# mLSTM cell inside a fused six-layer block: output banks copied by ScalarE, the causal mask taken out of TensorE's exponents

## The reference, cut to what matters

```
log_fg = log_sigmoid(fg); cs = cumsum(log_fg)
log_D[s, t] = cs[s] - cs_shift[t] + ig[t]      for t <= s, else -inf
D = exp(log_D - max_t log_D)
C = (q k^T / sqrt(DH)) * D
normaliser = max(|sum_t C|, exp(-max_log_D))
h = (C / (normaliser + 1e-8)) v
h_norm = (h - mean) / sqrt(var + 1e-5) * (1 + out_w)
x = layernorm(x + h_norm)
```

## Time and profile before

| | us |
|---|---|
| median of 3 runs | 1833.98 |
| lowest, highest | 1831.88, 1847.02 |
| profiled execution, its own time | 1832.67 |
| its span | 1830.9 |
| busy TensorE / VectorE / ScalarE / GpSimd | 1626.3 / 1176.4 / 683.8 / 312.8 |
| mLSTM unit loop in it, TensorE | 1094.4 to 1167 |
| covariance and bias matmuls | 1167 to 1187 |

### The profile page before, as it was taken

How to read it: one execution, slowest core, us unless ns; L and a number is a source line. 1 busy time by engine, 2 the same in 40 slices (tenths; PEclk the granted TensorE clock), 3 DMA queues, 4 the chain that set the end, 5 groups by cost and what they waited for, 6 DMA issues and landing times. The chain is left out here.

```text
span 1830.9 us, 38607 instructions
## 1 busy us (share of the span) xinstructions
PE 1626.3 (89%) x14748; PEld 1273.9 (70%) x14748; DVE 1176.4 (64%) x3829; ACT 683.8 (37%) x1425; POOL 312.8 (17%) x329
## 2 busy tenths in 40 slices
PE   6899987899997678898988869898899999999998
PEld 4677765666655556677776647776788888788876
DVE  3555664455554725566555636548888889889894
ACT  3333331246555246656555533323222223222210
POOL 1443435200000110000112105601010001000100
PEclk9899998999999868999998986799999999999999
DMA  3100000000010278989989970230000000000000
GB/s 125 47 18 18 18 18 13 18 19 25 25 54 30 87 258 301 327 281 326 319 299 330 333 237 16 95 141 2 1 8 8 13 2 13 13 2 13 2 7 13
DMA packets 98502, 177.36 MB, mean 97 GB/s; under 512 B 16144, under 2 KB 82832, under 8 KB 93584
## 3 DMA queue, kind: packets, MB, share of 16 engines
q1 hardware_dynamic: 98320, 174.89, 27.6%
HBM read 92.94 MB, written 81.79 MB: 95 GB/s over the span
## 5 line engine op out<-in xcount | busy, mean ns | idle before, releaser
L104 PE MATMUL bank<-per_xT,per_down 128*128 128x256 f32 x1024 | 250.5, 390 | 2.3 <-ACT per_xT L2625 1.6
L2946 PE MATMUL bank<-per_up,per_act_w 128*128 128x256 f32 x1024 | 242.3, 382 | 0.0
L2946 PEld LDWEIGHTS bank<-per_up,per_act_w 128*128 128x128 f32 x1024 | 195.3, 191 | 27.0
L2632 ACT ACTIVATE per_act_w<-bank 128x512 f32<-128x512 f32 x128 | 76.3, 598 | 364.0 <-PE bank L104 329.5
L104 PEld LDWEIGHTS bank<-per_xT,per_down 128*128 128x128 f32 x1024 | 190.2, 192 | 29.9 <-issue 2.7
L1503 ACT ACTIVATE rel_probs<-later_shared,rel_low 128x256 f32<-128x256 f32 x256 | 117.0, 518 | 27.4 <-DVE rel_low L1587 27.3
L1587 DVE CUSTOM_DVE_ANT_0 later_shared<-bank,later_shared 128x256 f32<-128x256 f32 x256 | 95.0, 419 | 37.0 <-DMA later_shared<-rel_qr_rows 18.9
L920 DVE TENSOR_REDUCE xat_mx<-bank 128x2 f32<-128x512 f32 x128 | 79.4, 683 | 32.7 <-PE bank L968 32.7
L104 PE MATMUL bank<-ret_x2T,ret_w_in 128*128 128x256 f32 x384 | 93.0, 399 | 7.5 <-issue 7.5
L2612 POOL TENSOR_TENSOR per_sim<-per_sim,per_best_i 128x512 f32<-128x512 f32 x32 | 41.9, 1330 | 332.6 <-DVE per_sim L2750 332.6
L1722 PE MATMUL bank<-rel_band_k,later_shared 32*128 32x191 f32 x512 | 64.6, 374 | 31.1 <-DVE rel_low L1587 23.8
(11 more groups left out here) (362 smaller groups left out, 3194.6 us busy)
## 6 DMA issues: line engine op xcount, KB each, us to landing
rel_qr_rows<-later_shared SPq DMA_DIRECT2D x32, 1024.0 KB, 8.4
rel_p_rows<-rel_probs SPq DMA_DIRECT2D x32, 1024.0 KB, 6.8
later_shared<-rel_qr_rows SPq DMA_DIRECT2D x64, 384.0 KB, 4.7
rel_by_dist<-rel_p_rows SPq DMA_DIRECT2D x64, 384.0 KB, 4.7
per_down<-in_per_down SPq DMA_DIRECT2D x1, 4096.0 KB, 12.8
per_up<-in_per_up SPq DMA_DIRECT2D x1, 4096.0 KB, 13.0
ret_xin<-in_x SPq DMA_DIRECT2D x8, 256.0 KB, 2.8
xat_cT<-in_contextT SPq DMA_DIRECT2D x8, 256.0 KB, 2.9
```

Of the source, the lines that this page charges most:

```text
L104: last = pe.matmul(dst, wt[:, c], src[:, c, :], start=c == 0, stop=c == DC - 1)
L2632: nc.scalar.activation(act_w[m % 2][:, 2 * k:2 * k + 2, :], tiles(bank[3 + k % 2]), ACT.Gelu_apprx_tanh).then_inc(gelu_ready, 1)
L2946: last = pe.matmul(tiles(bank[7])[:, t, :], act_w[n % 2][:, k, t * P:t * P + P], up[:, k, :], start=k == 0, stop=k == COLS - 1)
```

## The change

- The mask: `mask`, `mask16` and `ident16` go, and with them the two mask matmuls of each unit and ScalarE's two conversions. A table `limit` comes in, 3e38 on and below the diagonal and 0 above, and VectorE takes the minimum of decay and limit on the diagonal squares (128x512 a unit, both inputs in SBUF), ahead of line 2192.
- The outputs' banks: ScalarE copies them to `h` in SBUF, one instruction of 128x260 a bank (`take_of`, step 2b + 2), and TensorE's next outputs wait for `h_taken`, bank 6 and bank 7 apart. VectorE's normalisation reads h: its pairs of instructions (one for each bank) become one each, five in all, and it is done in step 2b + 3. All later per-batch steps move by one as well.
- h lies where `v_in` and `v_sum` lay (`values`), whose use is over by then.
- The sixth layer's steps beside the mLSTM layer are moved with it: the centre from step 7 to 9, beta_wide from 9 to 10, the centrings from step 8 and on to 9 and on, the reads of x by one step. BESIDE and STEPS are one step longer.
- The DMAs of the two tables are issued with the gates' (five under one semaphore, in place of three and two).

```diff
@@ mlstm_layer, streams
-    STEPS = range(-1, UNITS + 6)
+    STEPS = range(-1, UNITS + 7)
+    def take_of(s):
+        return batch(s - 2)
     def norm_of(s):
-        return batch(s - 2)
+        return batch(s - 3)
...
@@ scalar
-            if k == 4:
-                act.wait_ge(exact_loaded, 16 * len(exact_loads))
-                nc.scalar.activation(ident16[:], ident[:], ACT.Copy)
-                nc.scalar.activation(mask16[:], mask[:], ACT.Copy)
...
+            if (b := take_of(s)) is not None:
+                act.wait_ge(h_mm, HP * (b + 1))
+                if b >= 2:
+                    act.wait_ge(hn_part, b - 1)
+                for t in range(TT):
+                    nc.scalar.activation(h[:, b % 2, t], h_bank(t), ACT.Copy).then_inc(h_taken, 1)
@@ vector
                 dve.wait_ge(decay_ready, U + 1)
+                own = decay[:, U % 2].rearrange("p k (c s) -> p k c s", s=P)[:, :, 0:3:2]
+                dve.tensor_tensor(own, own, limit[:].unsqueeze(1).broadcast_to([P, HP, 2, P]), ALU.min)
+                dve.drain()
                 dve.wait_ge(qk_mm, U + 1)
...
-                dve.wait_ge(h_mm, HP * (b + 1))
+                dve.wait_ge(h_taken, TT * (b + 1))
...
-                for t in range(TT):
-                    dve.scalar_tensor_tensor(out=norm[:, t], in0=h_bank(t)[:, :, DH], scalar=-1.0,
-                                             in1=percol[:, 1, t, NH * b:NH * b + NH],
-                                             op0=ALU.mult, op1=ALU.max)
+                dve.scalar_tensor_tensor(out=norm[:], in0=h[:, b % 2, :, :, DH], scalar=-1.0,
+                                         in1=percol[:, 1, :, NH * b:NH * b + NH], op0=ALU.mult, op1=ALU.max)
                 dve.drain()
-                for t in range(TT):
-                    dve.tensor_tensor(norm[:, t], h_bank(t)[:, :, DH], norm[:, t], ALU.max)
+                dve.tensor_tensor(norm[:], h[:, b % 2, :, :, DH], norm[:], ALU.max)
...
-                for t in range(TT):
-                    last = dve.tensor_tensor(hn[:, b % 2, t], h_bank(t)[:, :, 0:DH], over(norm[:, t], DH), ALU.mult)
-                last.then_inc(hn_part, 1)
+                dve.tensor_tensor(flat(hn[:, b % 2]), flat(h[:, b % 2])[:, :, 0:DH],
+                                  over(norm[:].rearrange("p t h -> p (t h)"), DH), ALU.mult).then_inc(hn_part, 1)
@@ tensor
             for k in range(HP):
-                pe.matmul(d_bank(U, k)[:, 0:SPAN], minus[:, NH * b + HP * pair + k], m_parts[:],
-                          start=True, stop=False)
-                behind = d_bank(U, k)[:].rearrange("p (t s) -> p t s", t=TT)[:, :, 0:P]
-                last = pe.matmul(behind, ident16[:], mask16[:], start=False, stop=True)
+                last = pe.matmul(d_bank(U, k)[:, 0:SPAN], minus[:, NH * b + HP * pair + k], m_parts[:],
+                                 start=True, stop=True)
...
-            if b >= 1:
-                pe.wait_ge(hn_part, b)
             for k in range(HP):
+                n = HP * pair + k
+                if b >= 1 and n == 0:
+                    pe.wait_ge(h_taken, TT * b - 1)
...
+                if b >= 1 and n == 0:
+                    pe.wait_ge(h_taken, TT * b)
...
@@ peer_layer
-    BESIDE = range(-1, 2 * nb + 6)
+    BESIDE = range(-1, 2 * nb + 7)
...
-            if s >= 8 and s % 2 == 0:
-                if s == 8:
+            if s >= 9 and s % 2 == 1:
+                if s == 9:
                     pool.wait_ge(centre_ready, 1)
...
-            if s == 7:
+            if s == 9:
                 dve.wait_ge(centre_mm, 1)
```

More of the change, by code:

```diff
@@ L1880, in sem @@
         return nc.alloc_semaphore("mls_" + name)
-    mask, diag = early("mask", [TT, P]), early("diag", [R], rows=PARTS)
-    ident16, mask16 = early("ident16", [P], BF16), early("mask16", [TT, P], BF16)
+    limit, diag = early("limit", [TT, P]), early("diag", [R], rows=PARTS)
     w_gate, b_gate = early("w_gate", [3, DC, 2, NH]), early("b_gate", [2], rows=LINES)
@@ L1928, in mlstm_layer @@
                                                   sem("decay_ready"))
-    qk_mm, c_ready, h_mm, hn_part, sq_ready = (sem("qk_mm"), sem("c_ready"), sem("h_mm"), sem("hn_part"),
-                                               sem("sq_ready"))
+    qk_mm, c_ready, h_mm, h_taken, hn_part, sq_ready = (sem("qk_mm"), sem("c_ready"), sem("h_mm"), sem("h_taken"),
+                                                        sem("hn_part"), sem("sq_ready"))
     hvar, hrstd, hn_ready, out_ready, var, rstd, y_ready = (sem("hvar"), sem("hrstd"), sem("hn_ready"),
                                                             sem("out_ready"), sem("var"), sem("rstd"), sem("y_ready"))
-    gate_loads = [(w_gate[:], w["w_gate"]), (b_gate[:], w["b_gate"]), (select[:], w["select"])]
-    exact_loads = [(mask[:], w["mask"]), (diag[:], w["diag"])]
+    gate_loads = [(w_gate[:], w["w_gate"]), (b_gate[:], w["b_gate"]), (select[:], w["select"]),
+                  (limit[:], w["limit"]), (diag[:], w["diag"])]
     rest_loads = [(out_w[:], w["out_w"].partition_broadcast(P))]
-    STEPS = range(-1, UNITS + 6)
+    STEPS = range(-1, UNITS + 7)
     def unit(k):
@@ L1944, in batch @@
         return k // HP if k % HP == 0 and 0 <= k // HP < nb else None
+    def take_of(s):
+        return batch(s - 2)
     def norm_of(s):
-        return batch(s - 2)
+        return batch(s - 3)
     def var_of(s):
-        return batch(s - 3)
+        return batch(s - 4)
     def scale_of(s):
-        return batch(s - 4)
+        return batch(s - 5)
     def stats_of(s):
-        return batch(s - 5)
+        return batch(s - 6)
     def end_of(s):
-        return batch(s - 6)
+        return batch(s - 7)
     def flat(ap):
@@ L2040, in gpsimd @@
                 pool.wait_ge(v_centred, b)
-            pool.tensor_tensor(v_sum[:], values[:, :, 0:wide], values[:, :, wide:DH], ALU.add)
+            pool.tensor_tensor(v_sum, own[:, :, 0:wide], own[:, :, wide:DH], ALU.add)
             pool.drain()
@@ L2048, in gpsimd @@
             pool.drain()
-            pool.tensor_tensor(values, values, over(v_sum[:, :, 0], DH), ALU.subtract).then_inc(v_centred, 1)
+            pool.tensor_tensor(own, own, over(v_sum[:, :, 0], DH), ALU.subtract).then_inc(v_centred, 1)
             yield
@@ L2313, in outputs @@
                 pe.wait_ge(v_ones, 1)
-            if b >= 1:
-                pe.wait_ge(hn_part, b)
             for k in range(HP):
-                h = HP * pair + k
-                pe.matmul(h_bank(0)[:, h], c[:, U % 2, k, 0:P], v[:, b, 0, h], start=True, stop=True)
-                pe.matmul(h_bank(1)[:, h], c[:, U % 2, k, P:256], v[:, b, 0, h], start=True, stop=False)
-                last = pe.matmul(h_bank(1)[:, h], c[:, U % 2, k, 256:SPAN], v[:, b, 1, h], start=False, stop=True)
+                n = HP * pair + k
+                if b >= 1 and n == 0:
+                    pe.wait_ge(h_taken, TT * b - 1)
+                pe.matmul(h_bank(0)[:, n], c[:, U % 2, k, 0:P], v[:, b, 0, n], start=True, stop=True)
+                if b >= 1 and n == 0:
+                    pe.wait_ge(h_taken, TT * b)
+                pe.matmul(h_bank(1)[:, n], c[:, U % 2, k, P:256], v[:, b, 0, n], start=True, stop=False)
+                last = pe.matmul(h_bank(1)[:, n], c[:, U % 2, k, 256:SPAN], v[:, b, 1, n], start=False, stop=True)
             last.then_inc(h_mm, 1)
@@ L2358, in outputs_read @@
     def outputs_read(engine):
-        engine.wait_ge(hn_part, nb)
+        engine.wait_ge(h_taken, TT * nb)
     yield dict(sync=sync, gpsimd=gpsimd, scalar=scalar, vector=vector, tensor=tensor), dict(
@@ L2583, in gpsimd @@
         for s in BESIDE:
-            if s >= 8 and s % 2 == 0:
-                if s == 8:
+            if s >= 9 and s % 2 == 1:
+                if s == 9:
                     pool.wait_ge(centre_ready, 1)
-                for n in ((0, 1) if s == 8 else (s // 2 - 3,)):
+                for n in ((0, 1) if s == 9 else (s // 2 - 3,)):
                     pool.tensor_tensor(xc[:, n, :, 0:D], before["result"](pool, n),
@@ L3087, in mlstm_arrays @@
     key, query = np.arange(P)[:, None], np.arange(P)[None]
-    behind = np.where(key > query, np.float32(-1e30), np.float32(0))
+    limit = np.where(key > query, np.float32(0), np.float32(3e38))
     lines = heads * BATCHES
@@ L3097, in mlstm_arrays @@
         "mls_select": select.reshape(P, P),
-        "mls_mask": np.stack([behind, behind], 1),
+        "mls_limit": np.stack([limit, limit], 1),
         "mls_diag": np.tile(np.eye(lines, dtype=np.float32), (3, 1)),
```

15 lines of the change are left out of this document (9 added, 6 removed).

## The result

The kernel before took 1832.58 us (median of 12 runs, 1825.84 to 1847.02), the changed one 1840.82 us (12 runs, 1837.09 to 1846.45): a ratio of 1.0048, 95% interval 1.0027 to 1.0069. That is slower, by 8 us, and within 1%. The profiled execution of the changed kernel took 1845.36 us with a span of 1843.6, 12.7 more than the span before.

The account below looks back on a forecast made before the run. TensorE was taken to bound the loop at two clocks, with VectorE late at the high one. Loop 0.2, tail 5.2 and clock behind it 3 gave +8.4 us: 1832.67 becomes 1841.1 profiled, 1842 as median, range 1829 to 1850.

Parts of the forecast that it names:

- Mask matmuls, 5.22 to 4.80 us a step: TensorE in the unit loop at 1.2 GHz: dropping two mask matmuls of 0.21 us takes a step from 5.22 to 4.80.
- Minimum, 0.76 a unit on the path: VectorE's new minimum in each step: 0.68 us and 0.08 for the drain, on the path because VectorE will be late.
- the third rival: Minima on VectorE also held up by GpSimd, 2.5 us a batch: +21 us, 1855; chance 0.06.
- Copies at nothing, four stalls gone: ScalarE's bank copies, 0.8 us a batch, cost nothing; TensorE's four waits at batch ends, 5.6 us, go.
- Normalisation held up, 3.6 to 4.0 us for 1.7: VectorE's normalisation chain out of SBUF waits for GpSimd's two products for y: 3.6 to 4.0 us, floor 1.7.
- the first rival: No hold-up that matters between GpSimd and VectorE; VectorE's batch is 7.9: -6 to +0.5 us, about 1831; chance 0.22.
- I expect VectorE to set the pace at 10.0 whatever the clock: Unit loop: VectorE's batch of 10.0 us, held up, exceeds TensorE's 9.6 at the low clock and 4.8 at the high.
- the loop's sum of +0.2: Loop to the end of unit 15's product with the scores: 1162.9 where before it was 1162.7, +0.2 us.
- the signs that the prediction named for the loop: Steps of some 5 us with VectorE, not TensorE, without gaps; no wait of TensorE for a bank.
- Tail, +5.2: Behind the loop, the deeper pipeline ends centred batch 6 22.1 us after unit 15's product, against 16.9: 5.2 later.
- Clock behind the tail, +3 of 0 to 7.1: TensorE idles ahead of batch 6, so its clock falls for the work behind: +3 us, between +0 and +7.1.
- The second rival: Loop as before, tail hidden because TensorE at a low clock comes late to batch 6: +0 to +4, about 1836; chance 0.12.

Follow-up runs that it names:

- e6: The changed kernel with the minimum on VectorE done twice in each unit; 1849.05 us, ratio 1.0096 to the kernel before.
- e1: The changed kernel with the mask back on TensorE and no minimum; ScalarE's copies and the deeper pipeline stay; 1835.89 us, ratio 1.0046 to the kernel before.
- e8: The changed kernel with the mask back on TensorE, no minimum, and VectorE's normalisation ahead of the scale; 1834.66 us, ratio 1.0007 to the kernel before.
- e4: The changed kernel with VectorE's normalisation placed ahead of the scale in its step, depth unchanged; 1838.82 us, ratio 1.0051 to the kernel before.
- e5: The changed kernel with the mask matmuls added again on TensorE beside the minimum, so the mask is applied twice; 1844.92 us, ratio 1.0076 to the kernel before.
- e3: The changed kernel with the normalisation back in the step of the copies and later steps one earlier; 1838.65 us, ratio 1.0055 to the kernel before.

## Why the prediction came out as it did

The time was right (1842 predicted, 1840.82 measured, well inside 1829 to 1850). The mechanism was right in the tail and wrong in the loop: there a loss of 0.2 us was summed, for another reason than the trace shows, and the two profiles of the changed kernel have 5.3. The profile that the sum described came out 4.3 us longer (1845.36 for 1841.1); the second profile of the same kernel (1841.61) differs from the first only ahead of the stage. That the medians differ by 8.2 us, as summed (+8.4), is therefore in part luck.

**Mask matmuls, 5.22 to 4.80 us a step:** right, 4.79.

**Minimum, 0.76 a unit on the path:** the duration was right (0.684 and the drain), its place on the path wrong. TensorE never waited for VectorE's c in the loop, so the minimum cost at most a part of the 1.3 us by which VectorE was late at the end. A second minimum costs nothing in units 1 to 4 and about three quarters of itself later (e6). None was held up, so the third rival fell.

**Copies at nothing, four stalls gone:** right for the changed kernel. A copy took 0.365 to 0.407 us, and no wait for a bank is left. The cover that the prediction saw at the high clock, the 0.92 us of the next products, was not enough in e1: behind products of 0.92 TensorE waited for the copies in three places, 2.9 us in all.

**Normalisation held up, 3.6 to 4.0 us for 1.7:** right in the mechanism, 3.38 in the batch shown; undisturbed it is 1.68 (e8). That was the first rival's question. Taking the hold-up away gained 1.3 us in the loop (e4), where the rival had 2 to 8.5; in the tail it gained, with the new order, 3.0, where the rival had 2.7.

**"I expect VectorE to set the pace at 10.0 whatever the clock", and the loop's sum of +0.2:** this step failed. TensorE set the pace, at 4.79 us a unit or 9.59 a batch, busy for 71.31 of 71.89 us; of the signs that the prediction named for the loop, steps with VectorE and not TensorE without gaps, the trace shows the opposite. VectorE's batch was a little shorter than 10.0 (9.5 by e6, an estimate), and above all the clock was not what the sum took it to be. The sum let the first steps run at two clocks as before and had unit 5's product with the scores at 1110.8. It began at 1114.48, 3.7 us late. From there to unit 15's it took 51.70 us where 51.1 were predicted, but of other parts: five batches of TensorE at 9.59, 2.5 for the centre, and the 1.3 by which VectorE came to be late. That the two agree to 0.6 us is luck, since VectorE's 10.0 and TensorE's 9.59 lie so close. So the 4.3 us between E as predicted (1162.9) and as measured (1167.2) arose for the most part in the first five units, where the high clock was missing. I had taken the clock's pattern for a given; in the changed kernel it was another, and with the mask matmuls back it rose again in the one execution of e5 that was profiled.

**Tail, +5.2:** right, +5.6, and by its steps too: the last product of batch 7's chain ended at E+12.9 (predicted 12.4), centred batch 6 at E+22.55 (22.1). e3 shows that it goes with the depth, and e4 that 3.0 of it go with the order on VectorE.

**Clock behind the tail, +3 of 0 to 7.1:** right in kind, +2.2.

**The second rival, hidden in a slack of TensorE:** not what happened; TensorE waited 2.32 and 3.86 us in the tail. Why the medians differ by 8.2 and the two profiles by 12.7 is not shown. The stage alone is 13.2 and 13.3 us longer in the two profiles of the changed kernel than in the one of the kernel before. What lies ahead of the stage moved by 3.9 us between those two, in the same instructions, and whether the clock in the 66.56 us loop of the kernel before is typical of its runs can't be told from one profile.

What stays open besides: which property of the mask matmuls matters to the clock. They are bf16, they lengthen a unit's work, and they change where fp32 matmuls and short gaps fall; e5 put all of that back at once, in one profile, and no run varied them singly. Nor is the minimum ruled out as a second cause, as the means over runs say. Nor is it shown that the high clock is worth having in each kernel: e5 had it and was not faster.

## What to carry to other kernels

Before removing work from an engine whose clock has two levels, ask what the clock was in each stretch of the trace and whether the sum takes that pattern as given: here 0.43 us a unit were saved, and in the loop some 24 us at the high clock (an estimate from the mean of 0.68 over 66.56 us) were gone with them. A buffer that makes the pipeline a step deeper pays in the loop and costs in the tail: against e3 the changed kernel has 5.3 us less in the loop and 9.1 more behind it. Sum both ends. And when a chain moves from a bank into SBUF, look at which GpSimd instruction starts at the same moment; placing the chain one instruction group earlier took its hold-up away (3.38 to 1.68 us), though the median gained nothing that the intervals can tell.

## What the runs showed of the hardware

The granted clock stayed at 0.50 for 71.9 us, with TensorE busy 71.3 of them and never idle for more than 0.6 us, in both profiles of the changed kernel; the five other kernels without the bf16 mask matmuls had 0.50 throughout too, for 70.6 to 77.8 us. I had expected unbroken work to raise it, since before it had risen behind 8.4 us of it; the unbroken work of fp32 matmuls and bf16 distances alone did not raise it.

A VectorE instruction of 0.17 us with two SBUF inputs takes 1.21 to 1.22 us when it begins 0.07 us behind a GpSimd instruction of 1.26. A tensor_scalar of 0.17 us takes up to 1.29; where it began 0.04 us ahead of GpSimd's instruction it stayed at 0.17 (1117.55 and 1117.59). The reciprocal stayed at 0.20 in all eight batches, though it began under a GpSimd instruction of 1.26 in five of them.
